# A five-layer attention and mixture-of-experts kernel on one core: inverse sums taken at their own places, three chunks' expert rows prepared at the end of the search

## What is computed

```python
x = x + _attn(_ln(x, ln1_w[l], ln1_b[l]), ...)   # causal, 16 heads of 8
h = _ln(x, ln2_w[l], ln2_b[l])
moe = _token_moe if l % 2 == 0 else _seq_moe
x = x + moe(h, gate_w[l], gate_b[l], e_w1[l], e_b1[l], e_w2[l], e_b2[l])
```

## Time and profile before

| | us |
|---|---|
| runs of the kernel (3) | 3233.05, 3234.84, 3238.23 |
| median | 3234.84 |
| the profiled execution | 3232.04 |
| its span, first to last instruction | 3230.3 |
| mean granted TensorE clock | 0.91 of full |
| TensorE, VectorE, ScalarE, GpSimd busy | 83%, 80%, 70%, 18% |

### The profile page before, as it was taken

The page is one execution under the profiler, slowest core; times in us unless marked ns, Lnnn a source line. Parts: engine busy times, 40 slices in busy tenths (PEclk is TensorE's granted clock), DMA queues, the critical chain, the costliest instruction groups (busy, mean ns, idle before and its releaser), DMA issues. The chain is left out here.

```text
span 3230.3 us, 72067 instructions
## 1 busy us (share of the span) xinstructions
PE 2680.5 (83%) x28144; PEld 1172.3 (36%) x28144; DVE 2593.8 (80%) x3530; ACT 2271.0 (70%) x4360; POOL 590.0 (18%) x1119
## 2 busy tenths in 40 slices
PE   4468998899599985759999998489997997899976
PEld 3322332577323323412222222232332775333325
DVE  5669998577699985669999998389996775899966
ACT  1137897677378975439999998358896675588964
POOL 3123100444221001100000000132101443321011
PEclk8669999899699997869999999789998998799987
DMA  1071000211600000230000000240001212400001
GB/s 32 1 150 35 17 14 19 61 47 37 134 25 16 15 19 24 62 71 8 14 8 12 8 14 18 71 89 22 12 12 29 70 43 69 97 20 14 12 23 30
DMA packets 109758, 119.06 MB, mean 37 GB/s; under 512 B 20662, under 2 KB 87532, under 8 KB 109420
## 3 DMA queue, kind: packets, MB, share of 16 engines
q1 hardware_dynamic: 100780, 96.63, 11.1%
q0 software_dynamic: 4480, 13.90, 2.2%
q10 hardware_dynamic: 4160, 3.93, 0.6%
HBM read 70.31 MB, written 43.78 MB: 35 GB/s over the span
## 5 line engine op out<-in xcount | busy, mean ns | idle before, releaser
L1237 ACT ACTIVATE h_probsf<-h_ps_scoresf 128x512 f32<-128x512 f32 (+3 forms) x1216 | 603.7, 552 | 182.9 <-PE h_ps_scoresf L1183 170.4
L1237 ACT ACTIVATE h_probsg<-h_ps_scoresg 128x512 f32<-128x512 f32 (+3 forms) x1216 | 603.8, 552 | 169.8 <-PE h_ps_scoresg L1183 157.3
L1237 ACT ACTIVATE h_probsb<-h_ps_scoresb 128x512 f32<-128x512 f32 x1024 | 556.4, 596 | 106.5 <-PE h_ps_scoresb L1183 96.7
L1205 PE MATMUL h_ps_valuesf<-h_probsf,v_all 128*9 128x256 f32 (+2 forms) x4608 | 352.6, 379 | 38.4 <-POOL h_probsf L1314 31.2
L1205 PE MATMUL h_ps_valuesg<-h_probsg,v_all 128*9 128x256 f32 (+2 forms) x4608 | 350.8, 377 | 28.3 <-POOL h_probsg L1314 20.9
L1205 PE MATMUL h_ps_valuesb<-h_probsb,v_all 128*9 128x256 f32 x4096 | 319.3, 384 | 9.2 <-ACT h_drainedb L1244 4.5
L1272 DVE TENSOR_REDUCE h_maxima_0b<-h_ps_scanb 128x2 f32<-128x1024 f32 x256 | 292.7, 1217 | 28.8 <-PE h_ps_scanb L1145 28.8
L1272 DVE TENSOR_REDUCE h_maxima_2b<-h_ps_scanb 128x2 f32<-128x1024 f32 x256 | 293.1, 1217 | 15.9 <-PE h_ps_scanb L1145 15.9
L1272 DVE TENSOR_REDUCE h_maxima_0f<-h_ps_scanf 128x2 f32<-128x1024 f32 x224 | 259.3, 1219 | 23.1 <-PE h_ps_scanf L1145 22.8
L1272 DVE TENSOR_REDUCE h_maxima_0g<-h_ps_scang 128x2 f32<-128x1024 f32 x224 | 259.2, 1219 | 21.0 <-PE h_ps_scang L1145 20.6
L1183 PE MATMUL h_ps_scoresf<-q_stack,k_stack 49*128 49x256 bf16 (+2 forms) x2048 | 229.7, 288 | 31.8 <-DMA q_stack<-h_shiftsf 19.5
(11 more groups left out here) (407 smaller groups left out, 4339.5 us busy)
## 6 DMA issues: line engine op xcount, KB each, us to landing
q_stack<-combine_weights SPq DMA_DIRECT2D x64, 256.0 KB, 3.1
q_stack<-in_L_ffn_e_w SPq DMA_DIRECT2D x24, 256.0 KB, 3.1
q_stack<-q_parts SPq DMA_DIRECT2D x20, 256.0 KB, 5.8
k_stack<-k_parts SPq DMA_DIRECT2D x20, 256.0 KB, 8.5
attended<-h_drainedf SPq DMA_DIRECT2D x16, 256.0 KB, 2.6
attended<-h_drainedf SPq DMA_DIRECT2D x32, 128.0 KB, 1.9
attended<-h_drainedb SPq DMA_DIRECT2D x32, 128.0 KB, 1.9
attended<-h_drainedg SPq DMA_DIRECT2D x16, 256.0 KB, 2.2
```

Of the source, the lines that this page charges most:

```text
L1205: last = nc.tensor.matmul(ps_values[32 * j:32 * j + VD, low:high], m.v_all[:, kb, QUAD * quad + j, :], probs[:, (u + j % banks) % RING_P, ...
L1237: nc.scalar.activation(by_head(probs[:, of % RING_P, :], of), by_head(ps_scores[:, of % RING_S, :], of), ACT.Exp, scale=SOFTMAX_SCALE).the ...
```

## The change

1. plan.invert_at becomes a table. Chunk c is inverted at the first scan of group ends[c] + 5, that is groups 8, 12, 20 (12, 20, 28 in the full layer), and Finish.spread is cut in two: spread (the write) and gather (wait and read back), which the plan places 3500 ns behind it.
2. Class Rows prepares the expert rows of chunks 0 to 2 inside attention_heads, at the end of the search: one set of moments for 12 tiles, three powers on GpSimd ahead of its last diagonal masks, normalise, a new TensorE piece "rows" (four turns into the scan's PSUM ring), and both parts and the difference on VectorE instead of ScalarE. The sequence layers sum the rows with a VectorE reduction instead of ScalarE's accumulator. The experts then start with logits(0) (by token) or with the projection of the last chunk (by sequence), and chunk 3 alone is prepared in the old way.
3. The choice is two halves, one before step 0 (by token) and one behind it; combine(0) comes at step 3 rather than 7, the turn of its weights at step 5 rather than 10.
4. Two w2 loads are issued ahead of the last attended write, GpSimd waits for the last attended writes before it splits, and its last three w2 splits stand behind the first three weightings. The last expert of the last chunk is weighed by VectorE from PSUM.
5. ScalarE runs one Gelu of one column ahead of the last drain, which loads the Gelu table there.
6. The semaphore clears stand behind the powers of the next projection.

The core of the diff:

```diff
         @block.gpsimd
         def _(pool):
-            m.clear(pool, "finish", "experts")
             inverse_root(nc, pool, m, m.rstd[:, :], tmp[:, 0, :], var_ready, rstd_ready, 1)
             if first:
                 inverse_root(nc, pool, m, scale[:, :], tmp[:, 0, :], var_ready, rstd_ready, 2)
+            m.clear(pool, "finish", "experts", "rows", "w2")
             buffers.pad(nc, m)
             load_stacks(pool, 1, 1)
...
+        if causal:
+            self.searched += [("rows", c) for c in range(CHUNKS - 1)]
         self.ends = [max(g for g, x in enumerate(self.groups) if x[0] == c) for c in range(CHUNKS)]
-        self.invert_at = min(i for i, x in enumerate(self.searched) if x[:2] == ("scan", len(self.groups) - 1))
+        self.invert_at = {min(i for i, x in enumerate(self.searched) if x[:2] == ("scan", self.ends[c] + INVERT_AFTER)): c
+                          for c in range(CHUNKS - 1)}
...
-                if n_scan == self.invert_at:
-                    vector += (CHUNKS - 1) * INVERT
-                    moves += [(vector, "spread", c) for c in range(CHUNKS - 1)]
+                if n_scan in self.invert_at:
+                    vector += INVERT
+                    moves += [(vector, "spread", self.invert_at[n_scan]),
+                              (vector + GATHER, "gather", self.invert_at[n_scan])]
...
+                elif x[0] in ("finish", "rows"):
+                    vector = max(vector, arrived) + (ADD if x[0] == "finish" else KEEP)
                     freed.append(vector + VECTOR_DONE)
+                    if x == ("finish", CHUNKS - 2):
+                        vector += MOMENTS
+                        normal = [vector + SCALE * c for c in range(CHUNKS - 1)]
...
+            def turn_rows(i, c):
+                pe.wait_ge(freed, i - RING_A + 1)
+                rows_of.turn(pe, c, ps_scan[:, i % RING_A, 0, :]).then_inc(searched, 1)
...
+                    if rows_of and of == len(groups) - 1:
+                        nc.scalar.activation(m.spare[:, :], m.ones[:, 0:1], ACT.Gelu)
                     act.wait_ge(valued, plan.last_step(of) + 1)
...
-                if i == plan.invert_at:
-                    for c in range(CHUNKS - 1):
-                        finish.invert(dve, c)
+                if i in plan.invert_at:
+                    finish.invert(dve, plan.invert_at[i])
...
+                    if rows_of and x[1] == CHUNKS - 2:
+                        rows_of.moments(Steps(dve, rows_of.steps), range(CHUNKS - 1))
+                        for c in range(2):
+                            rows_of.normalise(dve, c)
+                elif x[0] == "rows":
+                    rows_of.keep(dve, x[1], ps_scan[:, i % RING_A, 0, :])
+                    rows_of.split(dve, x[1], ps_scan[:, i % RING_A, 0, :]).then_inc(freed, 1)
+                    if x[1] == 0:
+                        rows_of.normalise(dve, 2)
...
+                if units[u][0] == len(groups) - 1 and units[on_diagonal[k - 1]][0] < len(groups) - 1:
+                    for c in range(CHUNKS - 1):
+                        rows_of.inverse_deviation(pool, c)
...
+                if w2 and k == len(plan.moves) - 1:
+                    for e in range(RING_W2):
+                        w2.load(sp, e)
+                {"shift": shift, "write": write, "sums": sums, "spread": finish.spread, "gather": finish.gather}[kind](sp, g)
...
+    def gather(self, sp, c):
+        cols = slice(c * CH, (c + 1) * CH)
         sp.wait_ge(self.inverse_out, 16 * (c + 1))
         sp.dma_start(self.inverse[c], self.m.r_dram[:, cols].unsqueeze(1).broadcast_to([HEADS, HD, CH]))\
...
-FIRST_LOGITS, FIRST_CHOICE, FIRST_COMBINED, FIRST_WEIGHTS = 3, 4, 7, 10
-LAST_INVERT, LAST_SCALE, LAST_PROJECT, LAST_ADD = 1, 5, 7, 8
+FIRST_COMBINED, FIRST_WEIGHTS, FIRST_ROWS, LATE_SPLITS = 3, 5, 3, 3
+LAST_INVERT, LAST_SCALE, LAST_PROJECT, LAST_ADD, LAST_MOMENTS = 1, 5, 7, 8, 10
 NORMALISE, TURN, LOGITS, CHOICE, COMBINED, WEIGHTS = 8, 12, 17, 18, 21, 24
 TURN_BACK = 7
...
-            for c in range(end):
-                inverse_deviation(c)
+            for done in attended["out"]:
+                pool.wait_ge(*done)
             if by_token:
-                for e in range(E):
-                    split_w2(e)
+                for e in range(E - LATE_SPLITS):
+                    second.split(pool, e, w2_hi, w2_lo)
                     if e == 1:
                         exponential(0)
-                    if e == 3:
-                        inverse_deviation(end)
             else:
-                inverse_deviation(end)
+                rows.inverse_deviation(pool, end)
                 exponential(0)
                 for e in range(TOPK):
-                    split_w2(e)
-            for y in range(CHUNKS * n_exp):
+                    second.split(pool, e, w2_hi, w2_lo)
+            for y in range(CHUNKS * n_exp - (1 if by_token else 0)):
...
+                    if y < LATE_SPLITS:
+                        second.split(pool, E - LATE_SPLITS + y, w2_hi, w2_lo)
+                    if y == LATE_SPLITS:
+                        rows.inverse_deviation(pool, end)
...
+            def weigh_last(y):
+                part = y_sb[:, y % 2, :]
+                dve.wait_ge(down_ready, total)
+                dve.wait_ge(cw_in[y % RING_CW], 16 * (y // RING_CW + 1))
+                dve.wait_ge(weighted, y - 1)
+                nc.vector.scalar_tensor_tensor(part, ps_y[:, y % 2, :], m.vecs[:, E_B2 + E - 1:E_B2 + E],
+                                               cw_rows[:, y % RING_CW, :], ALU.add, ALU.mult).then_inc(by_vector, 1)
+                dve.wait_ge(by_vector, 1)
+                dve.wait_ge(weighted, y)
+                nc.vector.tensor_tensor(acc[:, end % 2, :], acc[:, end % 2, :], part, ALU.add).then_inc(weighted, 1)
+
+            if by_token:
+                choose(0)
+            else:
                 finish.invert(dve, end)
                 finish.scale(dve, end)
-                split_h(2)
                 finish.add_last(dve, ps_end)
-                moments(end)
-                normalise_chunk(end)
-                split_h(end)
+                rows.moments(step, [end])
+                rows.normalise(dve, end)
+                rows.split(dve, end, ps_turn[:, end % 2, :]).then_inc(rows.h_split, 1)
                 choose_experts()
...
+                    if k == 0:
+                        choose_second(0)
                     if k == LAST_INVERT:
                         finish.invert(dve, end)
-                    if k == FIRST_CHOICE:
-                        choose(0)
+                    if k == FIRST_COMBINED:
+                        combine(0)
...
                     if k == LAST_ADD:
                         finish.add_last(dve, ps_end)
...
+                    if k == LAST_MOMENTS:
+                        rows.moments(step, [end])
+                    if prepared(k, NORMALISE) == end:
+                        rows.normalise(dve, end)
+                    if prepared(k, TURN + 1) == end:
+                        rows.split(dve, end, ps_turn[:, end % 2, :]).then_inc(rows.h_split, 1)
+                    for offset, do in ((CHOICE, choose), (CHOICE + 1, choose_second), (COMBINED, combine)):
...
+            if by_token:
+                weigh_last(CHUNKS * n_exp - 1)
...
+            pe.wait_ge(*attended["searched"])
+            if by_token:
+                logits(0)
+            else:
                 project_last()
-                turn(end)
+                turn_last()
                 mean_logits()
...
-                    if k == FIRST_LOGITS:
-                        logits(0)
                     if k == LAST_PROJECT:
                         project_last()
                     if k == FIRST_WEIGHTS:
                         turn_cw(0)
-                    for offset, do in ((TURN, turn), (LOGITS, logits), (WEIGHTS, turn_cw)):
+                    if prepared(k, TURN) == end:
+                        turn_last()
+                    for offset, do in ((LOGITS, logits), (WEIGHTS, turn_cw)):
...
+            if not by_token:
+                evacuate(CHUNKS * n_exp - 1)
 
         @block.sync
         def _(sp):
+            finish.spread(sp, end)
+            finish.gather(sp, end)
...
+                for e in range(RING_W2, E - LATE_SPLITS):
+                    second.load(sp, e)
...
+                        if 0 <= y - FIRST_ROWS < LATE_SPLITS:
+                            second.load(sp, E - LATE_SPLITS + y - FIRST_ROWS)
```

253 lines of the change are left out of this document (131 added, 122 removed).

## The result

| | before | after |
|---|---|---|
| median of 4 runs, us | 3233.95 | 3187.03 |
| from, to | 3232.59, 3238.23 | 3181.33, 3189.62 |
| profiled execution, its span | 3232.04, 3230.3 | 3188.68, 3187.0 |
| mean granted clock | 0.910 | 0.919 |

The account below looks back on a forecast made before the run. Bounds: softmax scores waiting for shift rows behind SyncE's stalls, and the way from attention to experts. Attention 26.4, tokens 26, sequence 5.2 and clears 5.1 make 62.7 us less than 3232.04: 3169.3, as median 3172, range 3155 to 3200.

Parts of the forecast that it names:

- the case that was forecast: Whole kernel: median 3172 us, alone 3164 to 3181, with chance 0.48.
- first rival: Attention stall moves, rows and order cost more: attention gives 13, tokens 20, total 42 less, 3193 us; chance 0.22.
- Inverse sums: Attention: stall at the shift row goes; 8.1 in f0 and f1, 9.6 in g0 and g1, 7.4 in b.
- second rival: SyncE stalls at fifteen places instead of five, 5.3 us each, 80 us added: 3252 us; chance 0.03.
- Rows in the last group: Last group of each causal layer: a wait of 1.3 and turns of 1.4 cost 2.7 us per layer.
- third rival: GpSimd's powers and splits stretched by VectorE, 10 us in attention and 2 by token: 3184 us; chance 0.12.
- Experts by token: Layers f0 and g0: 13 us less per layer, 26 in all, bounds 8 and 15 per layer.
- Choice in halves: Experts by token: splitting the choice priced at 0.1 us and left out of the sum.
- TensorE hardly pauses, so it should stay at 2.4 GHz: First ups by token: 12 large products take 2.7 us, 3.9 less than before.
- The late stall of 3.8 us: Experts by token: ScalarE's evacuation wait for weightings behind eight w2 splits goes, with 1.6 us of low clock after it.
- fourth rival: More comes: no wait at the weights, rows hidden, clock high throughout, 77 us less, 3158 us; chance 0.12.
- Experts by sequence and clears: f1 and g1: 2.6 us less per layer, 5.2 in all; clears let powers start earlier behind f0, g0, f1: 5.1.

Follow-up runs that it names:

- e3: Before with the inverse sums at their own places and spread and gather apart, nothing else; 3190.58 us, ratio 0.9864.
- e9: After with VectorE's reduction of the expert rows over 8 columns instead of 512 (result incomplete); 3180.51 us.
- e10: e6 with the last chunk's scale, projection, addition and moments at steps 8, 11, 12, 14 instead of 5, 7, 8, 10; 3159.69 us, ratio 0.9781.
- e1: After with both halves of the choice at one step again for chunks 1 to 3; 3166.7 us, ratio 0.9790.
- e7: Before with only the choice in halves for chunks 1 to 3; 3250.03 us.
- e6: e1 with all w2 splits ahead of the weightings, loads for experts 2 and 3 earlier, first turn two steps later; 3166.61 us, ratio 0.9796.
- e8: Before with only the semaphore clears moved behind GpSimd's powers; 3232.01 us.
- e5: After with the first chunk's logits behind the fourth up product and the first choice at steps 1 and 2; 3182.47 us.

## Why the prediction was right or wrong

**The whole.** The range held and the case that was forecast did not: 3187 lies outside its own 3164 to 3181 and nearer the first rival's 3193. That nearness is luck. The first rival had attention give 13 us and the tokens 20, and they gave 28.7 and 1.5.

**Inverse sums: right, a little low.** 42.8 less 5.6 for the reciprocals was forecast, and e3 measured 42.5. In f0 (6.2 for 6.7) and g0 (8.4 for 8.2) the working holds; b gives 10.1 for 7.4. The charge for the reciprocals did not appear as such; the new order of scans took 3 us in its place, and the second stall gave 1.5 back through the clock, neither of which the prediction had. The second rival, SyncE stalling at fifteen places, did not occur.

**Rows in the last group: right, priced a little too low.** e3 to after is 13.8 us for four layers, 3.5 each for the 2.7 forecast (1.7, 3.7, 1.2 and 7.1 by layer, one execution each). In f0 it is the last group's 19.83 for 16.97 us. What was missed is the reduction in f1 and g1 (e9: about 1.4 each), which the prediction had charged to the experts as 0.5. GpSimd's powers were not stretched, so the third rival failed at the place that it named. Its ratio came from masks that ran beside one addition and three multiplications of VectorE.

**Experts by token: the failed step.** The term of 13 per layer measured next to nothing. Three of its parts failed; from after to e10, which has none of the first and third and projects the last chunk later, the two stretches lose 12.1 and 14.6 us.

- "Choice in halves: 0.1, left out" was the large one: 8.4 and 9.7 us by e1, 8.3 and 12.0 by e7. I had counted VectorE's instructions, which stay the same, and not asked who runs beside them. The exponential comes a step later, GpSimd works off its held-up weightings without a gap, and two of combine's five operations run among them at six times their length. This is the third rival's mechanism in the other direction: VectorE held by GpSimd.
- "TensorE hardly pauses, so it should stay at 2.4 GHz" was wrong in f0, by 5.3 - 3.2 = 2.1 us at the first four ups: it did not pause, and the clock fell all the same. In g0 it was right: the starts of the first and the last of these twelve products are 2.65 us apart, where 2.7 was forecast. Behind the last three turns of the weights the clock fell too, for 3 us or more each.
- The late stall of 3.8 us was to go with the three late splits. They brought one of their own, 4.3 us of waits for the low parts in f0, since their loads now queue behind the rows. Without them 0.8 is left in e6 and 2.1 in e10.

What was right there: the first turn waits 2.32 (3.0 forecast), the projection 1.1 (about 1.0), the tail 2.4 (1.9 left of 4.2). And e10, without the halves and the late splits, has the forecast 14 us, but as a total of other parts: its first turn waits 0.36 (3.0 forecast), and the clock falls at f0's first ups. It also stands at 3159.69, near the fourth rival's 3158 ("no wait at the weights"), which needed another kernel than this one.

**Experts by sequence and clears: right in size.** f1 to b lost 5.8 for the 4.5 forecast, and behind g1 2.2 for 2.6. The first gelu runs without a table load in front of it. The load now starts 0.02 us behind the last exponential and costs its 1.28, and no second wait stands beside it:

```profile
1227.30 1.28 ACT L1256 ACT_TABLE_LOAD   x1
...
1262.93 0.66 ACT L2012 ACTIVATE e_ps_hf<-e_ps_hf,q_stack 128x512 f32<-128x512 f32 x1 [12.72 <-PE e_ps_hf L1898]
```

The power behind f0 starts 0.07 us behind its variance (807.49 to 807.56). What e8's single run shows is 1.6 and 0.6 us in the token stretches and 0.9 in f1 to b. That is no more than the same code differs by between executions, so the earlier power is shown and the 5.1 for the clears is not.

**Left open.** Ahead of f0 and between b and g0 after is 3.6 and 1.8 us shorter, where the prediction had nothing. Ahead of f0 the kernels with the whole change take 201.2 to 203.9 us, before and those with one part (e3, e7, e8) 204.5 to 206.2. In before and after 1.0 of the 3.6 is there already in stage a, at 142 us, and the rest is two DMA waits that end sooner (2.07 to 1.12, and 4.09 to 2.48 for the first shift row). No instruction that the change moves stands at them, and whether it is more than the spread of single executions is not shown. The total forecast was 62.7 less on the profiled execution, 43.3 were measured, and 5.4 of these are this unexplained gain.

## What to carry to other kernels

Before a chain of short VectorE operations is moved, look at what GpSimd runs beside its new place: the chain's price is not its own length but that of the GpSimd operations of 512 columns that run beside it, up to once for each member. Reductions, reciprocals and what ran beside a GpSimd power paid nothing here. Splitting or delaying one link also delays GpSimd's answer, so the chain meets more of them. And a part whose price is "nothing" is worth one run alone: here such a part cost 20 us of a forecast gain of 62.

## What was not expected of the hardware

- VectorE operations of 0.19 us with two SBUF inputs took 0.94 to 1.27 beside GpSimd's 1.26 to 1.29, and all 28 short operations of after that were held ended within 0.05 of it. Beside a power of GpSimd (1.02) 36 of them, over all traces, kept their 0.19, and the power kept its 1.0 beside VectorE's normalisings.
- The granted clock fell to 1.2 GHz (0.57 over 586 to 594 us in f0 of after) with TensorE busy throughout, during products with 8 columns each. It did so in 8 of 14 such places and stayed at 1.00 in the other 6 (2454 to 2460 us in g0 of after); with products of 512 columns in the same place it stayed up in 4 of 4 (e5, 1.00 over 586 to 592).
